# GpSimd's squares wait for the next round's first row maxima

## The reference

```python
x = transpose(x, (0, 2, 3, 1)); shortcut = x
y = roll(layernorm(x, norm1), (-4, -4))              # windows of 8 x 8 tokens, shifted by 4
q, k, v = (windows(y) @ qkv_w.T + qkv_b), 6 heads of 16
attn = softmax(q * 16 ** -0.5 @ k.T + mask)          # mask: -100 across the image's seams
out = roll(unwindow((attn @ v) @ proj_w.T + proj_b), (4, 4))
x = shortcut + out
x = x + gelu(layernorm(x, norm2) @ mlp_w1.T + mlp_b1) @ mlp_w2.T + mlp_b2
x = transpose(x, (0, 3, 1, 2))
# divisive normalisation over channels (GDN)
out = x * rsqrt(einsum('nchw,ic->nihw', x * x, gamma_eff) + beta_eff)
```

## Time and profile before

| | |
|---|---|
| median of 3 runs | 1760.86 us (1759.41 to 1764.15) |
| profiled execution | 1759.48 us, of which the span of instructions is 1757.7 us |
| TensorE matmuls, busy | 1655.4 us, 94% |
| TensorE weight loads, busy | 1433.3 us, 82% |
| VectorE, busy | 1470.0 us, 84% |
| ScalarE, busy | 1511.9 us, 86% |
| GpSimd, busy | 366.2 us, 21% |
| DMA | 100.38 MB, mean 57 GB/s |

### The profile page before, as it was taken

How to read it: one execution, slowest core, us unless ns; L and a number is a source line. 1 busy time by engine, 2 the same in 40 slices (tenths; PEclk the granted TensorE clock), 3 DMA queues, 4 the chain that set the end, 5 groups by cost and what they waited for, 6 DMA issues and landing times.

```text
span 1757.7 us, 83088 instructions
## 1 busy us (share of the span) xinstructions
PE 1655.4 (94%) x33524; PEld 1433.3 (82%) x33524; DVE 1470.0 (84%) x4142; ACT 1511.9 (86%) x2957; POOL 366.2 (21%) x459
## 2 busy tenths in 40 slices
PE   5799999999999999999999999999999999999985
PEld 3688888888888888888888888888888888888874
DVE  5788888888888888888888888888888888888861
ACT  2689899898888998898898899998888988999873
POOL 2121221221221222222222222122122122122111
PEclk9999999999999999999999999999999999999997
DMA  2122222121122121221222222222212222212111
GB/s 57 48 56 57 55 63 61 55 67 55 54 68 55 54 68 56 58 63 57 61 60 57 61 59 57 66 55 58 66 53 61 64 54 64 59 55 67 34 34 32
DMA packets 179170, 100.38 MB, mean 57 GB/s; under 512 B 26869, under 2 KB 178791, under 8 KB 178791
## 3 DMA queue, kind: packets, MB, share of 16 engines
q1 hardware_dynamic: 178228, 94.96, 19.3%
q10 hardware_dynamic: 562, 0.11, 0.0%
HBM read 32.05 MB, written 25.17 MB: 33 GB/s over the span
## 4 chain that ended last, share of the span: by engine, by line
PE 58%; DVE 33%; issue 6%; DMA 1%; ACT 1%; SPq 0%; POOL 0%; DVEq 0%; POOLq 0%
PE mm_bank L1135 10%; DVE stats L739 8%; PE mm_bank L924 8%; PE score_banks L954 7%; PE pv_bank L1084 6%; DVE v_block L801 6%; PE mm_bank L1132 6%; DVE mean_gap L752 5%; PE mm_bank L922 4%; PE turn_banks L960 4%; PE mm_bank L1119 3%; DVE row_max L810 3%; DVE shifted L817 3%; PE score_banks L1098 3%; DVE y_lo L788 3%
## 5 line engine op out<-in xcount | busy, mean ns | idle before, releaser
L531 ACT ACT_TABLE_LOAD x256 | 328.4, 1283 | 4.6
L611 ACT ACTIVATE hidden<-mm_bank 128x512 f32<-128x512 f32 x384 | 229.4, 597 | 105.9 <-PE mm_bank L1119 93.9
L1132 PE MATMUL mm_bank<-hidden,w 128*32 128x384 f32 x2304 | 304.4, 498 | 0.0
L1135 PE MATMUL mm_bank<-hidden,w 128*32 128x128 f32 x2304 | 301.9, 277 | 0.0
L582 ACT ACTIVATE probs<-shifted 128x384 f32<-128x384 f32 x512 | 265.4, 519 | 40.0 <-DVE shifted L817 37.4
L1135 PEld LDWEIGHTS mm_bank<-hidden,w 128*32 128x32 f32 x2304 | 244.8, 111 | 1.5
L486 POOL TENSOR_TENSOR x<-x,b_bias 128x384 f32<-128x384 f32 x128 | 105.8, 827 | 668.0 <-PE turn_banks L946 668.0
L842 DVE TENSOR_TENSOR x<-mm_bank,x 128x384 f32<-128x384 f32 x128 | 71.4, 558 | 180.2 <-PE mm_bank L1135 180.2
L593 ACT ACTIVATE probs_t<-score_banks 128x512 f32<-128x512 f32 x384 | 215.0, 604 | 0.0
L817 DVE TENSOR_TENSOR shifted<-score_banks,row_max 128x384 f32<-128x384 f32 x384 | 199.8, 548 | 0.0
L810 DVE TENSOR_REDUCE row_max<-score_banks 128x6 f32<-128x384 f32 x384 | 199.7, 548 | 0.0
(11 more groups left out here) (110 smaller groups left out, 4529.8 us busy)
## 6 DMA issues: line engine op xcount, KB each, us to landing
x_ext<-in_x SPq DMA_DIRECT2D x128, 192.0 KB, 3.1
k_block<-k SPq DMA_DIRECT2D x256, 96.0 KB, 2.0
out<-o_ext SPq DMA_DIRECT2D x64, 192.0 KB, 2.4
x_ext<-in_x SPq DMA_DIRECT2D x128, 48.0 KB, 2.7
attended<-attended SPq DMA_DIRECT2D x384, 16.0 KB, 1.8
x<-x SPq DMA_DIRECT2D x384, 16.0 KB, 1.8
out<-o_ext SPq DMA_DIRECT2D x64, 96.0 KB, 2.3
out<-o_ext SPq DMA_DIRECT2D x128, 48.0 KB, 2.1
```

The lines of the kernel that those rows point to most:

```text
L531: nc.scalar.preload_act_table_set(name)
L611: nc.scalar.activation(hidden[:, n, :], mm_bank(f"mlp1_{n}", A)[:, :], ACT.Gelu)\
L1132: nc.tensor.matmul(to[group(j), 0:MAIN], w2[:, n, group(j)], hidden[:, n, 128:HALF], start=first, stop=last)
L1135: made = nc.tensor.matmul(to[strip, group(n, 128)], w2[:, c, group(n)], hidden[:, c, 0:128], start=c == 0, stop=c == HID_CHUNKS - 1)
```

## The change

The square is called one round later and as the first step of GpSimd's round, ahead of `bias_x`, and it waits in addition for the first maximum of that round. The count is capped for the last halves, after whose attention there are no more maxima.

```diff
@@ square(A)
                 wait_alone(pool, x3_ready, A + 1)
                 wait_alone(pool, x3_moved[A % 2], 16 * HEAD_PAIRS * (A // 2 + 1))
                 wait_alone(pool, den_made, A)
+                wait_alone(pool, max_ready, min(SCORE_GROUPS * (A - SETTLE + 1) + 1, SCORE_GROUPS * HALVES))
                 nc.gpsimd.tensor_tensor(x3_sq[0:DIM, :], x3[0:DIM, A % 2, :], x3[0:DIM, A % 2, :], ALU.mult)\
                     .then_inc(sq_ready, 1)
 
@@ GpSimd's steps(run, H)
 
+                run(square, SETTLE - 1)
                 run(bias_x, TURN_IN - 1)
                 run(wrap_out, DIVIDE)
                 run(wrap_x, TURN_IN + 1)
                 run(bias_x2, PROJECT)
-                run(square, SETTLE)
                 if H == -TURN_IN:
                     clear_blocks()
```

## The result

The changed kernel takes 1708.7 us (median of 4 runs, 1706.5 to 1713.3) against 1760.1 us (median of 4, 1755.4 to 1764.2) for the kernel before on the same chip: the ratio is 0.971, with a 95% interval from 0.968 to 0.974. The forecast was 1709 us.

The account below looks back on a forecast made before the run. TensorE and VectorE bound the kernel, each round set by when tiny instructions, held by GpSimd's square, are through. Span 1757.7 - 50.7 (stretch) - 1.3 (later rounds) = 1705.7, plus 1.8 and 1.4: 1709 us; range 1695 to 1730.

Parts of the forecast that it names:

- The hold: VectorE's tiny `mean_gap` (L752) is held until GpSimd's square ends: 0.729 us against 0.172 alone, 66 us over 119.
- The move alone costs nothing: Calling the square first in GpSimd's next round keeps the order of its work, so it costs nothing.
- The square at 1.77 and 1.95 us, its end at 2.81 and 2.99: GpSimd's square starts 0.18 us after the first maximum, 1.77 into even and 1.95 into odd rounds, ending 1.04 later.
- The cover of 0.07 us at no cost: Square lets TensorE's denominators go at 2.87 and 3.05 us, due at 2.94 and 3.12; costed at nothing.
- The rival of a thinner gain: Square 0.2 us later or pieces twice as often, each 14 to 16 us: 1725, both 1740; chance 0.12.
- Free rounds: Rounds with no tiny instruction held: medians 12.46 us even, 12.63 odd; at these the stretch takes 1492.8 us.
- The loss to extra pieces: Idle time without releaser, mostly inside TensorE's `times_v`: 0.12 us a round, some 14 us; gain 50.7 instead of 65.
- The tail: After the even stretch, past 1657.5 us: two or three long rounds should give another 1.3 us.
- The total: Whole kernel: span 1705.7 us plus 1.8 and 1.4, so 1709 us; 1700 to 1720 had chance 0.68.
- the clean case: Rival: the extra pieces in free rounds don't repeat, so 65 us is gained: 1695 us; chance 0.12.
- The slower case: Rival: GpSimd gets its turn only in VectorE's gaps, denominators load at 4.39 us: 1844 us; chance 0.05.
- the case of no change: Rival: something else holds L752, GpSimd's `bias_x2` being the candidate: 1761 us; chance 0.03.

Follow-up runs that it names:

- the fill of the same size: Kernel before, the square replaced at its old place by a GpSimd memset of the same 96x512 that reads nothing: 1701.06 us, ratio 0.966.
- the reductions: Kernel before, first two tiny VectorE instructions written as reductions with one strided SBUF input each, square left where it was: 1735.52 us in a single run.
- the halves: Kernel before, the square cut into two instructions of 96x256 at the old place: 1749.84 us, ratio 0.993.

## Why the prediction was right

By its own steps:

- **The hold.** Right, and now shown by experiments and not only read off one trace. In these runs the holder reads SBUF (the fill of the same size doesn't hold), the held one has two inputs there (the reductions aren't held), and the hold lasts to the end of one GpSimd instruction (the halves). The Trainium skill (SBUF — State Buffer, Who interferes with whom) says the same of GpSimd and a VectorE instruction with two SBUF inputs; the rows of the three experiments agree with it.
- **The move alone costs nothing.** Right: 0.9999.
- **The square at 1.77 and 1.95 us, its end at 2.81 and 2.99.** Measured 1.76 and 1.95, 2.80 and 2.99.
- **The cover of 0.07 us at no cost.** Right. With the square 0.59 us later the denominators loaded 0.50 later, so 0.09 us of it was cover; in the rows of the result the load comes 0.13 us after the square's end, of which 0.06 pass anyway. The rival of a thinner gain needed a square that comes late, and in the steady rounds it never does.
- **Free rounds.** Right: 12.45 and 12.63 in the median, for 12.46 and 12.63.
- **The loss to extra pieces.** The right size from a partly wrong sum. 60 x 12.45 + 59 x 12.63 = 1492.2 us would be clean, so 16.5 us are lost, for a forecast of 14. Of these, 3.5 us belong to six rounds that I had counted among the held ones. The 14 rounds with a piece in `times_v` are 8.1 us longer than clean ones in sum (forecast: 15 to 20 of them; before there were three, 2.1 us in sum). Most of the remaining 4.9 us are pieces too, in other places, which the prediction did not look for: 2.7 us in seven rounds whose weight loads of the denominators pause, 0.3 in a shorter pause of `times_v` in round 86, and 1.55 in a stop ahead of `times_v` in round 95. All nine end 1.3 to 1.5 us after a transfer of code. 0.4 us is left without a cause.
- **The tail.** 2.2 us for a forecast of 1.3. Single tails scatter by more than that: 100.2 us before and 94.8 with the call moved alone, which is no faster. So this neither bears the forecast out nor speaks against it.
- **The total.** 1708.7 us for 1709, closer than its parts: the stretch gained 1.6 us less than forecast and the tail 0.9 more, and single runs of the changed kernel span 6.8 us. That it meets to 0.3 us is luck; that it lies within a few us is not.

The stop in round 95 of the changed kernel lies in the key projection; the transfer before it ended at 1228.59.

```profile
1229.99 0.11 PEld L923 LDWEIGHTS mm_bank<-y,wk 97*32 97x32 f32 x1 [1.51 <-issue]
```

The miscounted six are rounds 30, 31, 62, 63, 94 and 95, the last row of windows of three images, in which every window has mask matmuls. The timeline of round 30 in the changed kernel:

```profile
402.08 0.16 PEld L1061 LDWEIGHTS score_banks<-k_block,q 32*64 32x64 f32 x6 [0.36 <-issue]
...
402.50 0.17 DVE L753 TENSOR_TENSOR mean_gap<-stats 128x8 f32<-128x8 f32 x1
...
403.77 0.56 DVE L811 TENSOR_REDUCE row_max<-pv_bank 128x6 f32<-128x384 f32 x1 [0.62 <-PE pv_bank L1069]
...
415.19 0.16 PEld L1061 LDWEIGHTS score_banks<-k_block,q 32*64 32x64 f32 x6 [0.36 <-issue]
```

The tiny instruction is free, and the maximum starts at 1.69 us all the same, because it waits for the masks; the round has 13.11 us. The same round of the kernel before reads

```profile
413.73 0.17 DVE L752 TENSOR_TENSOR mean_gap<-stats 128x8 f32<-128x8 f32 x1
...
415.00 0.56 DVE L810 TENSOR_REDUCE row_max<-pv_bank 128x6 f32<-128x384 f32 x1 [0.62 <-PE pv_bank L1068]
```

and is as long. In the other five a tiny instruction was held before, and freeing it gains nothing, because the maximum is late for the masks by nearly as much. My count took each late maximum for the work of a hold without looking at what else the maximum waited for. That made the gain 3.5 us too large: 3 x (13.12 - 12.45) + 3 x (13.12 - 12.63). The pieces, wherever they lie, and the rest came to 13.0 us, for 119 x 0.12 = 14.3, and the clean sum is 0.6 lower (1492.2 for 1492.8). So the stretch gained 3.5 - 1.3 - 0.6 = 1.6 us less than forecast, and the tail 0.9 more.

The rivals: the clean case, 1695 us, needed the pieces to stay away, and they came 14 times. By the Trainium skill (Runtime: NRT & Kernel Launch, Instruction fetch mechanics) code is fetched in blocks while the engine runs, and this is mostly hidden; the traces agree on the transfers and on pieces that go with the code, but here the pauses of 0.3 to 0.97 us from load to load in `times_v` are not hidden. No row names the transfer as what TensorE waited for; that it waited for the code is inferred, from the shift of the rounds and from the nearly constant time between the end of a transfer and the end of a pause. The slower case is out: the square ran beside the shift and the next maxima at its usual 1.04 us in every round. So is the case of no change. One reading of the prediction was slightly off: VectorE's next instruction with two SBUF inputs, L848, starts 6.87 us into the free round of the earlier trace rows, not past 7 us. The square is long through by then.

## What to carry to other kernels

When a tiny instruction's mean is several times that of its neighbours of the same size, look at what GpSimd reads in that time: a VectorE instruction with two SBUF inputs can stand for the whole of a GpSimd instruction, however small it is itself. The remedy is a wait, not a new order: let GpSimd start once VectorE has turned to work on PSUM, and count from there whether its result is still in time, since here one instruction later gives the gain back. Before rounds are counted as held, check what each late step would wait for without the hold, and take off something for waits for code that the removed stall had been hiding.

## What the hardware showed that I had not expected

- A 128x8 instruction of 0.17 us was held for 0.77 us, and a GpSimd fill of 96x512 (0.52 us) did not hold it at all.
- Two GpSimd instructions back to back hold two different victims: `within` went through between the halves, `gap_part` was caught by the second.
- The place of the pieces in `times_v` followed the place in TensorE's instruction sequence: with 128 more instructions ahead of it, none of its 15 rounds was among the 31 in which the eleven other traces had theirs. A second trace of the same kernel had only 8 of 14 rounds in common with the first.
- Each piece ended 1.2 to 1.6 us after the end of a 16 KB transfer on the instruction queue, 128 of 128.
- 128 semaphore increments on TensorE took 19.4 us, 0.15 us each, and put off its first full round by 14.1.
